# Expert layer of a graph network on one Trainium2 core: float32 products of high and low parts against scaled float16 pairs with rows transposed by DMA

## The reference

```python
def sage(h, src, dst, W_self, W_neigh, b):           # twice
    agg = segment_sum(h[src], dst, num_segments=6250)
    h_neigh = agg / maximum(degree, 1)[:, None]
    return relu(h @ W_self + h_neigh @ W_neigh + b)

def moe(xf, Wg, W1, b1, W2, b2, gamma, beta):        # 8 experts, 512 x 512 each
    topv, topi = top_k(xf @ Wg, 2); gate_w = softmax(topv)
    h = relu(einsum('td,edh->teh', xf, W1) + b1)
    y = einsum('teh,ehd->ted', h, W2) + b2
    y = (y - mean(y)) / sqrt(var(y) + 1e-5) * gamma + beta
    return sum(gate_w[:, :, None] * take_along_axis(y, topi[:, :, None], 1), 1)

x = x + two_sage_layers(layernorm(x))
x = x + moe(layernorm(x))
```

## Time and profile before

| | |
|---|---|
| runs | 2901.69 us median of 3 (2900.99 to 2908.44) |
| profiled execution | 2902.25 us, its span 2900.3 us |
| PE busy | 2395.9 us (83%) |
| POOL busy | 2005.5 us (69%) |
| DVE busy | 1567.2 us (54%) |
| ACT busy | 841.3 us (29%) |
| the chain that ended last, by engine | POOL 44%, PE 23%, issue 15%, DMA 11% |
| stages | set-up to 113 us, graph layers to 2160, expert tiles to 2872, end of the last tiles to 2900 |

### The profile page before, as it was taken

One profiled execution on the slowest core, in us unless ns is written; L12 is line 12 of the kernel. 1 busy time (PEld: TensorE's weight loads), 2 busy tenths in 40 slices (PEclk: granted clock), 3 DMA queues, 4 the chain that ended last, 5 costly groups with the idle time before them and its releaser, 6 DMA issues.

```text
span 2900.3 us, 55360 instructions
## 1 busy us (share of the span) xinstructions
PE 2395.9 (83%) x11308; PEld 1539.6 (53%) x11309; DVE 1567.2 (54%) x3789; ACT 841.3 (29%) x1611; POOL 2005.5 (69%) x2229
## 2 busy tenths in 40 slices
PE   1188888787888786888888888888988999999996
PEld 0044444444444443455555555554556778888885
DVE  8754454454454443354444444444546677777775
ACT  6512122111211111111111111111114555555554
POOL 0377777777777775777777777777745666666665
PEclk9998898989898999999999999999998999999998
DMA  7679988898987776888888888888875765666543
GB/s 272 231 234 303 303 301 297 298 306 297 312 293 244 231 233 201 277 263 255 257 250 260 255 258 252 259 256 259 261 219 133 162 140 119 141 138 134 106 80 62
DMA packets 239323, 663.61 MB, mean 229 GB/s; under 512 B 47224, under 2 KB 48818, under 8 KB 236168
## 3 DMA queue, kind: packets, MB, share of 16 engines
q0 software_dynamic: 151472, 464.79, 56.4%
q10 hardware_dynamic: 62388, 128.09, 12.4%
q1 hardware_dynamic: 25380, 69.89, 7.5%
HBM read 550.93 MB, written 111.69 MB: 228 GB/s over the span
## 4 chain that ended last, share of the span: by engine, by line
POOL 44%; PE 23%; issue 15%; DMA 11%; DVE 3%; ACT 2%; SPq 1%; POOLq 0%; DVEq 0%; ACTq 0%
POOL store_all L728 43%; PE ps L1767 19%; DMA store_all<-h_scratch,srcT 5%; DMA store_all<-xn_scratch,srcT 4%; PE ps L1932 1%; DMA wts<-expert_weights_scratch 1%; PE ps L1944 1%; ACT store_all L857 1%; SPq L394 1%; ACT ln_out L857 1%; DMA out<-store_all,idx_s 1%; PE ps L1797 1%; PE ps L1798 1%; DMA store_all<-in_L_gnn_W_self 0%; DVE wts L412 0%
## 5 line engine op out<-in xcount | busy, mean ns | idle before, releaser
L728 POOL DMA_INDIRECT store_all<-xn_scratch,srcT x782 | 778.8, 996 | 346.3 <-issue 227.2
L728 POOL DMA_INDIRECT store_all<-h_scratch,srcT x782 | 760.9, 973 | 256.4 <-issue 223.3
L1797 PE MATMUL ps<-store_all,sel 128*128 x1680 | 682.4, 406 | 300.2 <-SPq L616 285.1
L1798 PE MATMUL ps<-store_all,sel 128*128 x1680 | 672.3, 400 | 0.0
L1797 PEld LDWEIGHTS ps<-store_all,sel 128*128 128x128 f16 x1680 | 172.3, 103 | 666.6 <-issue 610.7
L1767 PE MATMUL ps<-wts,sT 128*128 128x512 f32 x1176 | 445.5, 491 | 0.8 <-DVE sT L1369 0.8
L1767 PE MATMUL ps<-wts,aT 128*128 128x512 f32 x1176 | 405.2, 454 | 0.8 <-DVE aT L1375 0.8
L1332 DVE TENSOR_TENSOR sel<-iota_g,dstT 128x384 f16<-128x384 f32 (+2 forms) x602 | 305.8, 525 | 37.5 <-issue 28.7
L1767 PE MATMUL ps<-wts,m_hT 128*128 (+1 forms) x1224 | 313.3, 405 | 4.2 <-DVE m_hT L1643 4.2
L1767 PE MATMUL ps<-wts,m_xT 128*128 (+1 forms) x1224 | 311.6, 403 | 4.9 <-DVE m_xT L1586 3.6
L1767 PEld LDWEIGHTS ps<-wts,sT 128*128 128x128 f32 x1176 | 238.7, 210 | 94.7 <-issue 38.3
(11 more groups left out here) (299 smaller groups left out, 3060.7 us busy)
## 6 DMA issues: line engine op xcount, KB each, us to landing
expert_weights_scratch<-w_both ACTq DMA_DIRECT2D x64, 512.0 KB
wts<-expert_weights_scratch SPq DMA_DIRECT2D x64, 512.0 KB, 4.9
store_all<-in_L_ffn_W ACTq DMA_DIRECT2D x64, 256.0 KB, 5.2
of_experts<-xn_scratch ACTq DMA_DIRECT2D x49, 256.0 KB, 5.3
of_experts<-h_scratch ACTq DMA_DIRECT2D x49, 256.0 KB, 4.1
store_all<-in_x ACTq DMA_DIRECT2D x49, 256.0 KB, 5.2
store_all<-xn_scratch,srcT POOLq DMA_INDIRECT x782, 4.5
store_all<-h_scratch,srcT POOLq DMA_INDIRECT x782, 4.1
```

What stands on the lines that cost most here:

```text
L728: pool.indirect_dma_start(rows[:, t % SLOTS, :], None, rows_d, bass.IndirectOffsetOnAxis(ap=srcT[:, t:t + 1], axis=0)).then_inc(s_rows[t % ...
L1797: pe.matmul(agg_p[p], sel[:, s, :], row[:, 0:D], start=k == 0, stop=False)
L1798: pe.matmul(agg_p[p], sel[:, s, :], row[:, D:2 * D], start=False, stop=False) \
```

## The change

- The experts' weights and rows become pairs of float16, scaled by powers of two so that the low halves keep their digits. Scales are found on the chip: in 16 tiles of layer 1 (4 to 19) DVE takes the largest and smallest value of a chunk of two blocks (`scan`), the partitions' bounds go through a small DRAM table, and DVE makes the scales (`own_bounds`, `weight_scales`). In 16 later tiles (24 to 39) the weights are loaded again, two blocks at a time, split (`expert_hi`, `expert_lo`) and stored as float16. `h_relu` and `add_b2` multiply by scales.
- Layer 2 stores the normalised rows as float16 pairs: `norm2` writes two copies, `norm_lo` on DVE makes the low half.
- In the expert stage the gathered float16 pairs (1024 columns) are transposed by a DMA on ACT's queue (`transpose_x`), from `m_x2` to one of two buffers `m_xT`. `x_t_m`, `x_hi` and `x_lo` go. `gather_x` waits for that DMA, no longer for PE.
- PE's order is `h_t_m(q - 1)`, `mm1(q)`, `mm2(q - 2)`; the norm of tile q - 3 runs beside tile q, and `m_hT` has two buffers. Gates and scatter come one tile later on POOL, and three tiles are finished after the last loop, where two were.
- An expert's weights take half the room: four DMAs of 512 KB, on layer 1's weights alone, so that experts 0 and 1 are both loaded at the start of layer 2.

```diff
@@ expert weights, SP
-                for k in range(KC):
+                for c in range(2):
                     for h in range(2):
-                        sp.dma_start(wts_e[:, par, k, h].bitcast(F32), wsplit_d[e * KC + k, :, h] ...
+                        sp.dma_start(wts_e[:, par, c, h].rearrange("p m b n -> p m (b n)"), wsplit_d[e * 2 + c, :, h] ...
...
                     load_expert(0, 0)
+                    load_expert(1, 1)
...
-            sp.wait_ge(L[1]["dense"], NT)
-            load_expert(1, 1)
@@ POOL
             def tile_m(q, half, pair):
-                gather_x(q + 3, 1 - half)
-                gather_gates(q, half)
+                gather_x(q + 3, 1 - half, pair + (1 + half))
+                if not isinstance(q, int) or q >= 1:
+                    gather_gates(q - 1, 1 - half)
                 next_rows(q + 4, half, pair * 16 + 32)
+                if not isinstance(q, int) or q >= 3:
+                    scatter(q - 3, 1 - half)
...
@@ ACT
-            def x_hi(q):
-                act.wait_ge(M["xT"], q + 1)
-                act.wait_ge(M["h"], q)
-                act.activation(m_xT[:, 0].rearrange("p k n -> p (k n)"), mxT_p, ACT.Copy).then_inc(M["xHi"], 1)
+            def transpose_x(half, landed):
+                alone(act, M["x"][half], landed)
+                act.dma_start_transpose(m_xT[:, half], m_x2[:, half]).then_inc(M["xT"][half], 16)
...
-            def tile_m(q):
+            def tile_m(q, half, pair):
                 if not isinstance(q, int) or q >= 1:
                     h_relu(q - 1, 0 if isinstance(q, int) and q <= LEAST else expert_of_last(q))
-                    h_hi(q - 1)
-                if not isinstance(q, int) or q >= 2:
-                    m_sqrt(q - 2)
+                    h_hi(q - 1, 1 - half)
+                if not isinstance(q, int) or q >= 3:
+                    m_sqrt(q - 3)
                 h_copy(q)
-                if not isinstance(q, int) or q >= 2:
-                    m_norm(q - 2)
-                x_hi(q + 1)
+                if not isinstance(q, int) or q >= 3:
+                    m_norm(q - 3)
+                transpose_x(half, pair * 16 + 32)
@@ ACT and DVE, layer 2
+                    for to in (pair[:, 0:D], xn2_t):
+                        i = act.activation(to, x2_t[:], ACT.Identity, bias=nmr[:, 0:1], scale=rstd[:, 0:1])
...
+                def norm_lo(n, p):
+                    dve.wait_ge(S["xn2"], n + 1)
+                    dve.tensor_tensor(pair[:, D:2 * D], xn2_t, pair[:, 0:D], ALU.subtract).then_inc(S["xnlo"], 1)
@@ DVE, layer 1
+                def scan(c, p):
+                    alone(dve, s_wraw, c * 32 + 32)
+                    for t, op in ((scan_max, ALU.max), (scan_min, ALU.min)):
+                        i = dve.tensor_reduce(out=t[:, bass.ds(c, 1), :].rearrange("p a m -> p (a m)"), in_=raw_chunk[p],
+                                              axis=AX.X, op=op)
+                    i.then_inc(s_scan, 1)
@@ DVE, experts
-                dve.tensor_tensor(m_yb, my_p, of_expert(0, e), ALU.add).then_inc(M["yb"], 1)
+                dve.scalar_tensor_tensor(out=m_yb, in0=my_p, scalar=y_sc[:, 0:1], in1=of_expert(0, e),
+                                         op0=ALU.mult, op1=ALU.add).then_inc(M["yb"], 1)
...
-                x_lo(q + 1)
@@ PE
+            def product_m(out_ap, w, lhs):
+                for k in range(KC):
+                    for a, b in ((0, 0), (1, 0), (0, 1)):
+                        i = pe.matmul(out_ap, lhs(a, k), w(b, k), start=k == 0 and (a, b) == (0, 0),
+                                      stop=k == KC - 1 and (a, b) == (0, 1))
+                return i
...
                 pe.wait_ge(s_wset, e + 3)
-                mm1(q, weights_of(e))
-                x_t_m(q + 1, 1 - half, pair * 16 + (16 + half * 16))
-                if not isinstance(q, int) or q >= 1:
-                    mm2(q - 1, weights_of(e_before))
+                mm1(q, weights_of(e), half, pair * 16 + 16)
+                if not isinstance(q, int) or q >= 2:
+                    mm2(q - 2, weights_of(experts_of(q - 1)[1]), half)
```

More of the change, by code:

```diff
@@ L513, in layer @@
             for g in range(head):
[L514 to L517 removed]
+                tile(g, g % 2, between.get(g, {}))
+            loop0 = head
+            for g0, n, more in early:
+                for g in range(loop0, g0):
+                    tile(g, g % 2, between.get(g, {}))
+                pairs(g0, g0 + n, more)
+                loop0 = g0 + n
             loop1 = loop0 + (NT - 2 - loop0) // 2 * 2
```

334 lines of the change are left out of this document (210 added, 124 removed).

## The result

| | before | after |
|---|---|---|
| median of the runs, us | 2901.34 (4 runs, 2900.68 to 2908.44) | 2960.13 (4 runs, 2952.82 to 2967.96) |
| profiled execution: time, span, us | 2902.25, 2900.3 | 2959.24, 2957.4 |
| granted TensorE clock over the span | 0.948 | 0.921 |

What follows compares the result with a forecast made beforehand. PE bounded the expert stage at 6.65 us a tile; DVE's and ACT's loop would become the bound at 6.02, saving 63 us over 100 tiles: 2902.25 - 63 + 3 - 1 = 2841 us, range 2808 to 2935.

Steps and rivals of the forecast that it cites:

- The products: PE, expert stage: 24 float16 products 0.22 us apart, 5.28, plus h transposes 0.44, make 5.72 us a tile.
- The DVE loop: DVE and ACT, expert stage: without `x_lo` the loop falls from 6.34 to 5.97, with the scale in `add_b2` 6.02 us.
- 4.0 + X: ACT's loop per tile, X the transpose's hold, 0.46 to 2.0 us; hidden under 2.0, no gain from 2.65.
- rival (a): Slower, expert stage: issuing the transpose holds ACT; at X = 3.8 a tile takes 7.8, kernel 3017 us; chance 0.15.
- Rival (c): DMA engines: scatter landing goes from 4.9 to 6.3 us or more, tile 6.4 to 6.65, kernel 2880 to 2905; chance 0.20.
- Rival (b): Crossbar: transpose occupies its stream longer than a tile, PE's `mm1` waits; tile 9.8, kernel about 3217 us; chance 0.08.
- Rows: Row gathers, expert stage: two tiles' time, 12 us, to land before ACT needs them, against a landing of 4.9 or less.
- Layers at 0: Layers 1 and 2: added DVE and ACT work is covered by POOL's gathers, 0 us; 69 us if the cover failed.
- The end: Epilogue: second products two tiles behind cost one more tile, between 0 and 6 us; 3 taken.
- Expert 1's earlier weights: SP: expert 1's weights no longer wait for layer 2's end, saving PE's one wait for weights, 1.2 us; 1 taken.

Runs made afterwards that it cites:

- e_token_hold: Changed kernel with three DMAs of 64 to 128 bytes on ACT's queue in place of each transpose from the third tile on: 2923.01 us, tile 6.69 us.
- e_beta: Changed kernel with `plus_beta` of a tile moved into the next tile's wait for `m_norm`, transposes kept: 3002.74 us, tile 7.35 us.
- e_early: Changed kernel with the DMA transpose issued right behind `h_hi` instead of behind `m_norm`: 2974.54 us, tile 7.05 us.
- b_pe: Changed kernel with x transposed by TensorE (eight float16 blocks) and one ACT copy, no DMA transpose: 2901.16 us, tile 6.45 us.
- e_token: Changed kernel with a 128-byte DMA on the same queue in place of each transpose from the third tile on: 2901.02 us, tile 6.40 us.
- e_noload: Changed kernel where DVE does not read a tile's expert out of `tab_use` but uses fixed rows: 2952.02 us, tile 6.98 us.
- e_load_only: Changed kernel with transposes between unused tiles, issued behind `h_hi`, no waits for rows or landing, and no DVE expert register load: 2902.23 us, tile 6.45 us.
- e_one: Changed kernel with second products one tile behind again: 2956.88 us, tile 7.01 us, end 35.5 us.
- b_split: Changed kernel with rows stored and gathered as float32, transposed by TensorE, split by ACT and DVE, `plus_beta` moved into `m_norm`'s wait: 2884.30 us, tile 6.38 us.

## Why the prediction was wrong

The step that failed is the loop through DVE and ACT, taken as the bound at 6.02 us a tile. It was counted without the register work, branch and register load in DVE's and ACT's own streams, and with a DMA transpose that ACT would hide. The tile measured 6.99 us: 0.38 more without any transpose, and 0.59 more with them.

**The products: right.** Twelve take 2.59 to 2.60 us, 0.22 apart; with h's transposes a tile needs 5.63 us of PE (5.72 forecast). `h_lo` stayed at 0.66 to 0.69 us and `add_b2` took 0.75 (0.74 forecast). PE was no longer the bound, as forecast.

**The DVE loop, 5.97 to 6.02 us: wrong by 0.38.** The step was: without `x_lo`, beta follows gamma by 0.15, and the next `add_b2` follows beta as in the earlier trace rows. Measured without the transposes: 6.40 us. `x_lo` had covered DVE's own register work ahead of `plus_beta`, and the earlier trace rows show one tile of a loop that holds two; the branch stands at the end of the other, where the first of these rows has 0.52 us of "issue" against 0.21 in the last.

**"4.0 + X" on ACT, X up to 2.0: the size was wrong, and rival (a) was at work.** The hold itself was in my range, 1.26 us at the median. But behind it in the same stream come the loop's branch, the register load for the next tile (0.80 us at the median, 0.28 before) and the address work, which used to run while ACT waited: 2.45 us a tile from `m_norm` to `h_relu` on average. About 0.2 of these are a wait for gathered rows, which I had ruled out: 17 of 99 transposes start late by it, 22 us in all. `h_relu` with a scale takes 0.36 us more as well (1.50 against 1.14). 4.0 + 2.45 + 0.36 = 6.8 us by estimate, past the break-even that I had set at X = 2.65. That rival was priced at 7.8 us; in e_token_hold a longer hold by itself cost 0.29 us a tile.

**Rival (c), the DMA engines: at work too, with 0.22 us a tile.** Landings of 6.3 to 6.8 us stand in the chain, as that rival had it, but they are the long ones: where the profile gives a median for the scatter beside transposes it is 4.8 to 5.5 us (e_beta, e_early). The transposes act on more than the scatter: register loads take longer too, but only at certain times. In the ten kernels with a transpose for every tile of the stage, register loads of a tile's expert that began 1.0 to 3.5 us after a transpose was issued took 0.70 us at the median (1706 loads), the others 0.30 (1273). So DVE's load, 0.62 us after, took 0.31 in e_beta and 0.30 in e_early, where it falls at other times. **Rival (b)** did not happen as priced: PE waited 7 times for a transpose between 2250 and 2850 us, 13.9 us in all.

The Trainium skill's 1309 ns for a block through the crossbar (VectorE: DVE Perf Modes, The three transpose paths) would be 10.5 us for eight, an estimate; a transpose landed in 5.3 us at the median and the tile was 6.99. The 261 GB/s of the Trainium skill (DMA: Bandwidth & Descriptors, Latency and other measured facts), 1.0 us by estimate, is off on the other side, and by more: 256 KB in 5.3 us are 49 GB/s, landing included. The rule of the first of these pages of the Trainium skill to use TensorE where PSUM will do holds here: b_pe is 59 us faster than after.

**The sum for a tile:** 6.02 forecast + 0.38 (loop) + 0.29 (hold) + 0.22 (load) + 0.09 (waits for landings) = 7.00; measured 6.99. That the two agree so well is luck: the terms are from separate runs and need not add. The hold was 1.8 us in e_token_hold, the load was measured on a loop without DVE's register load, and 0.09 is within the spread. What is shown is the 0.38 (e_token) and the 0.59 for the transposes together (e_token, b_pe); how the 0.59 divide is argued.

DVE's own order gives another reading of the same 0.59, which the sum leaves out. Its idle time ahead of `add_b2` in the table of waits from 2250 to 2850 us (us in total, times, longest us), after and then in e_token:

```profile
DVE store_all L1769 <- issue: 80.5, 85, 2.0
```

```profile
DVE store_all L1773 <- issue: 53.2, 94, 0.9
```

That is 0.95 us a wait against 0.57. By estimate the longer register load alone (0.62 us at the median against 0.31) makes DVE's loop 6.40 + 0.38 = 6.8 us, as long as ACT's by the estimate above. In e_noload DVE's load is gone, and the tile stays at 6.98 with DVE waiting for ACT. In e_load_only DVE's load is gone and the transposes stand where ACT waits anyway, and the tile falls to 6.45 with as many transposes. So two loops of about the same length are the likely reason why a cure of one of them gave nothing; e_early and e_beta bring a wait for gathered rows besides.

**Rows.** "A gather has two tiles' time to land before ACT needs it" failed: ACT needs the rows of tile q + 2 at the end of tile q, one tile sooner than PE did, and everything on ACT stands behind that wait (e_early, e_beta, and 17 times in the changed kernel itself).

**Layers at 0: wrong in layer 2, by about 20 us in this pair of traces.** I had counted the work of `norm_lo` as covered by POOL's gathers, but not asked whether the two hinder each other. Layer 1, with its scan and its larger loads, was right at 0.

**The end, 0 to 6 us, 3 taken:** 7.5, over the range by 1.5, of which 6.2 go to the extra tile behind (e_one).

What stays open: why the first product comes 15.3 us later when the last gather is 20.4 us later. From the last gather to the first product every changed kernel takes 41.3 to 46.8 us, b_split with its float32 rows 42.6, where the kernel before takes 47.5, so neither the float16 rows nor the DMA transposes are the reason. Expert 1's earlier weights (1 us forecast) were not tried apart. Of the load's 0.22 us the late scatters are a part (e_load_only); whether the row gathers land later by it is not shown.

## What to carry to other kernels

When a change takes the bound off one engine, time the next loop with every instruction of its stream in it, register loads, branches and DMA issue too, over the whole loop body: such work is free only as long as the engine waits anyway. A DMA that is issued by an engine in a serial loop can cost that loop its issue time (0.29 us a tile here), and its wait for inputs is a wait of everything behind it. When several loops are about equally long, taking one off shows nothing. An instruction that is off the path can still slow the one that paces a stage, so look at what runs beside it.

## What was not expected of the hardware

- Register loads of one number from SBUF took 0.62 to 0.80 us at the median on DVE and ACT in the changed kernel, 0.28 to 0.31 us before. The long ones began 1.0 to 3.5 us after a transpose was issued; at other times beside the same transposes the median was 0.30 us.
- A `tensor_tensor` of DVE over 512 columns with both inputs in SBUF held an indirect gather on POOL at 1.95 us in place of 0.95; with 16 columns in place of 512 the layer's gathers took 23 us less.
- A DMA transpose of 128 x 1024 float16 from SBUF to SBUF held ACT for 1.26 us at the median and landed after 5.3 us; a plain copy of the same bytes held it for 0.48 us and landed after 4.2.
